# Head maxima subtracted on TensorE, small GpSimd work moved, FFN rounding on the way out of PSUM, and new order tables

## The chip, the core and the metric

The kernel runs on one core of one Trainium2 chip. The metric is device time in microseconds (us). A core has five instruction streams that run beside each other and meet only at semaphores: TensorE (PE, matmuls; its weight loads are listed apart as PEld), VectorE (DVE), ScalarE (ACT), GpSimd (POOL), and SyncE (SP), which here only issues DMAs.

## What is computed

The input is 16 batches of 128 tokens x 128 channels, with a context of the same shape. Four layers follow one another, each added to the running `x` behind a tanh gate. The first is an attention whose softmax runs over the 16 heads (`axis=1`), not over the keys, so every score has to be divided by a sum over heads. The second is a mixture of 8 experts of which each token uses two (the kernel computes all eight and weighs them). The third attends to the context with three kinds of products and joins four pieces through `W_l`. The fourth is an FFN whose activations are rounded to whole numbers up to 127 and whose weights are rounded to -1, 0, 1.

```python
# layer 1 (16 heads of 8 channels)
score = jnp.einsum('bhij,bhkj->bhik', k, q) / jnp.sqrt(jnp.asarray(dh, k.dtype))
attn = jax.nn.softmax(score, axis=1)
out = jnp.einsum('bhik,bhij->bhjk', attn, v)
...
# layer 3
x = jnp.concatenate([c, c2q_att, c * c2q_att, c * q2c_att], axis=-1)
z = x @ W_l.T + b_l
...
# layer 4
scale = 127.0 / jnp.clip(jnp.max(jnp.abs(x), axis=-1, keepdims=True), 1e-05)
xq = jnp.clip(jnp.round(x * scale), -128.0, 127.0) / scale
```

## The kernel before

The work is cut into 8 pairs of two batches (256 tokens). A pair goes through the four layers, whose tiles and steps begin with `a_` (and `head_`), `m_`, `f_` and `g_`. What each engine does, and in which order, is written out by hand: the table `WHEN` gives every step of every pair a number, `ONCE` the steps that run once, and `order(engine)` sorts an engine's steps by them. The engine walks that list from front to back; semaphores hold a step until its inputs are there. A step that waits therefore holds everything behind it on its engine. The numbers interleave the pairs: the attention of one pair stands among the experts of the pair before, the third layer of that one, and the FFN of the one before it.

Scores are made in four units to a pair, each 128 keys x 16 heads x 64 queries, and each fills both banks of the one PSUM tile `ps_sc`. For one unit: PE makes 16 small matmuls (L1234); DVE takes the maximum over heads (`head_max`, L1584) and subtracts it on the way to SBUF (`shifted`, L1590), which sets `s_shift` and so frees `ps_sc` for the next unit; ACT takes the exponential (`attn`, L1046); POOL adds up the heads as a tree of four steps (L939); DVE takes the reciprocal (L1606); POOL multiplies (L945); PE forms the weighted values (L1196). For units 1 and 3 of pair 0, DVE adds up the heads instead (L1598).

The rows of queries and keys that L1234 reads go through DRAM: SP stores three bf16 parts of each (L791) and then fetches them back as `k_rows` and `q_rows` (L799); the first unit of a pair waits for both.

The expert tiles are made by L1188 to L1190 (three fp32r products of 256 columns per tile), a GELU-like activation on ACT and DVE, and L1448. Every layer norm ends in `rstd()` on POOL: four instructions on 128x2 values (L843, L844, L846, L848). POOL also turns the two best experts into probabilities (`top_probs`, L885 to L894), and forms `y_res` = `y` + the bias of `W_l` (L912) which L1728 adds to the third layer. In the FFN, ACT adds a large constant `ROUND` that makes the float round (`g_r` L1143, `g_pr` L1165), a second pass takes it off and writes bf16 (`g_q` on DVE, L1750; `g_pq` on ACT, L1172), PE transposes these (L1373, L1399), and ACT copies them out of PSUM (`g_qt` L1152, `g_pt` L1181). The last pair has no work of a next pair beside it. Spare matmuls that feed nothing (L1205, L1213) stand at the start and at the end.

## Time and profile before

| | |
|---|---|
| Time, median of 3 runs | 398.3 us (397.81 to 398.43) |
| Span of the profiled execution | 397.3 us |
| Busy: PE / DVE / ACT / POOL | 324.9 / 313.1 / 256.4 / 299.1 us |
| Chain that ended last, share by engine | PE 37%, POOL 25%, DVE 13%, issue 10%, ACT 7%, DMA 4%, SP queue 3% |
| First transposes of the experts' input (L1243), pair 0 and pair 7 | 56.2 and 333.4 us |

The span runs from the first to the last instruction of one profiled execution. Busy times add up what an engine spent in instructions; those of PE overlap each other, because matmuls are pipelined. The chain is followed back from the last instruction, at each step to what released it. The last line gives the beat of the loop: seven periods lie between pair 0 and pair 7.

### The profile page before, as it was taken

To read this page: it belongs to the slowest core of one execution; us is meant where nothing else is said; L and a number is where in the kernel's file an instruction comes from. 1 tells how busy PE (TensorE), PEld (TensorE's weight loads), DVE (VectorE), ACT (ScalarE), POOL (GpSimd) and SP (SyncE) were. 2 spreads that over 40 slices of the span, in tenths; PEclk is the share of its full clock that TensorE was granted. 3 is DMA by queue.
4 is the path that set the end of the run, shared out by engine and by line. 5 is a ranking of instruction groups with operands and counts; after the bars stand their busy time and mean duration, and the time that the engine had idled before them with its cause. 6 is when DMAs were issued, how large, how long until landed. Compare 5 with 4: busy or idle time off the path is not lost.

```text
span 397.3 us, 10407 instructions
## 1 busy us (share of the span) xinstructions
PE 324.9 (82%) x3326; PEld 284.0 (71%) x3326; DVE 313.1 (79%) x913; ACT 256.4 (65%) x726; POOL 299.1 (75%) x459
## 2 busy tenths in 40 slices
PE   1365589898999789979998899879978997996875
PEld 1255469787898679867986698669957896994742
DVE  2679877598869997999799979995989678778434
ACT  4335254536846797779667885777658855875754
POOL 4378989799898989898999799988778873443010
PEclk9999767999999999999999999998999999999585
DMA  5967210300341114012401221204100000000000
GB/s 161 289 192 210 81 36 21 116 17 16 88 115 34 29 41 128 19 56 63 108 15 47 68 87 29 61 6 131 33 16 1 28 15 2 2 29 14 2 13 13
DMA packets 34454, 24.17 MB, mean 61 GB/s; under 512 B 3617, under 2 KB 32097, under 8 KB 34401
## 3 DMA queue, kind: packets, MB, share of 16 engines
q1 hardware_dynamic: 33680, 23.32, 19.7%
q8 instruction: 27, 0.44, 0.5%
q10 hardware_dynamic: 720, 0.20, 0.2%
q14 instruction: 27, 0.21, 0.2%
HBM read 16.16 MB, written 7.34 MB: 59 GB/s over the span
## 4 chain that ended last, share of the span: by engine, by line
PE 37%; POOL 25%; DVE 13%; issue 10%; ACT 7%; DMA 4%; SPq 3%; POOLq 0%; DVEq 0%; ACTq 0%
POOL tree L939 9%; PE ps_d L1448 8%; POOL attn L945 8%; PE ps_z L1188 4%; PE ps_a L1196 3%; PE ps_z L1189 3%; PE ps_z L1190 3%; POOL m_h L876 2%; DVE head_max L1584 2%; DMA wf_raw<-in_wd 2%; DVE m_u L1623 1%; DMA k_rows<-rows_dram 1%; DVE y L1655 1%; PE ps_sc L1234 1%; DVE shifted L1590 1%
## 5 line engine op out<-in xcount | busy, mean ns | idle before, releaser
L1188 PE MATMUL ps_z<-m_xhi,w_hi 128*128 128x256 f32 x240 | 76.9, 320 | 12.7 <-DVE m_h L1631 6.1
L945 POOL TENSOR_TENSOR attn<-attn,head_inv 128x1024 f32<-128x1024 f32 x32 | 75.8, 2371 | 0.2 <-DVE head_inv L1606 0.2
L1448 PE MATMUL ps_d<-wdn,m_h 128*128 128x128 f32 x512 | 71.4, 283 | 4.7 <-DVE m_h L1631 2.1
L1448 PEld LDWEIGHTS ps_d<-wdn,m_h 128*128 128x128 f32 x512 | 63.1, 194 | 8.5 <-issue 4.1
L1189 PE MATMUL ps_z<-m_xhi,w_lo 128*128 128x256 f32 x240 | 68.8, 287 | 0.0
L1190 PE MATMUL ps_z<-m_xlo,w_hi 128*128 128x256 f32 x240 | 68.6, 286 | 0.0
L1623 DVE SCALAR_TENSOR_TENSOR m_u<-m_tanh,ps_z 128x256 f32<-128x256 f32 x120 | 49.0, 411 | 17.6 <-ACT m_tanh L1033 16.7
L1033 ACT ACTIVATE m_tanh<-ps_z 128x256 f32<-128x256 f32 x120 | 45.9, 384 | 26.0 <-PE ps_z L1190 25.6
L1188 PEld LDWEIGHTS ps_z<-m_xhi,w_hi 128*128 128x128 f32 x240 | 46.7, 195 | 19.3 <-issue 6.1
L876 POOL TENSOR_TENSOR m_h<-m_u,m_z 128x256 f32<-128x256 f32 x56 | 41.1, 734 | 17.2 <-DVE m_u L1623 17.2
L939 POOL TENSOR_TENSOR tree<-tree 128x256 f32<-128x256 f32 (+2 forms) x90 | 46.4, 515 | 7.1
L1189 PEld LDWEIGHTS ps_z<-m_xhi,w_lo 128*128 128x128 f32 x240 | 46.9, 196 | 0.0
L1190 PEld LDWEIGHTS ps_z<-m_xlo,w_hi 128*128 128x128 f32 x240 | 46.7, 195 | 0.0
L939 POOL TENSOR_TENSOR tree<-attn 128x512 f32<-128x512 f32 x30 | 38.3, 1277 | 6.5 <-ACT attn L1046 6.3
L1584 DVE TENSOR_REDUCE head_max<-ps_sc 128x64 f32<-128x1024 f32 x32 | 38.9, 1215 | 4.5 <-PE ps_sc L1234 4.2
L1046 ACT ACTIVATE attn<-shifted 128x1024 f32<-128x1024 f32 x32 | 33.7, 1055 | 10.1 <-DVE shifted L1590 10.1
L1590 DVE TENSOR_TENSOR shifted<-ps_sc,head_max 128x1024 f32<-128x1024 f32 x32 | 38.8, 1213 | 0.3
L1655 DVE SCALAR_TENSOR_TENSOR y<-ps_d,weights,y 128x128 f32<-128x128 f32 x96 | 28.8, 342 | 4.5 <-PE ps_d L1448 3.1
L1631 DVE TENSOR_TENSOR m_h<-m_u,ps_z 128x256 f32<-128x256 f32 x67 | 27.6, 414 | 5.8 <-PE ps_d L1448 5.1
L1031 ACT ACTIVATE m_z<-ps_z 128x256 f32<-128x256 f32 x53 | 20.2, 381 | 14.6 <-PE ps_z L1190 13.8
L1196 PE MATMUL ps_a<-attn,v_diag 128*32 128x128 f32 x512 | 20.4, 290 | 3.7 <-POOL attn L945 3.3
L1234 PE MATMUL ps_sc<-q_rows,k_rows 48*128 48x64 bf16 x512 | 13.7, 196 | 7.7 <-DVE shifted L1590 5.6
(311 smaller groups left out, 852.0 us busy)
## 6 DMA issues: line engine op xcount, KB each, us to landing
rows_dram<-qk_parts SPq DMA_DIRECT2D x16, 192.0 KB, 2.2
k_rows<-rows_dram SPq DMA_DIRECT2D x16, 192.0 KB
q_rows<-rows_dram SPq DMA_DIRECT2D x16, 192.0 KB
w_raw<-in_w SPq DMA_DIRECT2D x2, 1024.0 KB, 7.9
rows_dram<-qk_parts SPq DMA_DIRECT2D x16, 128.0 KB, 2.0
x_in<-in_x SPq DMA_DIRECT2D x8, 128.0 KB, 2.4
ct_in<-in_ctx_t SPq DMA_DIRECT2D x8, 128.0 KB, 2.4
rows_dram<-qk_parts SPq DMA_DIRECT2D x16, 64.0 KB, 1.7
```

What stands on the lines that cost most here:

```text
L876: pool.tensor_tensor(m_h[:, k % 4], m_u[:, k % 4], m_z1[:, n % 3], ALU.mult).then_inc(s_mhp, 1)
L939: pool.tensor_tensor(dst, src[:, 0:n, :], src[:, n:2 * n, :], ALU.add).then_inc(s_tree, 1)
L945: pool.tensor_tensor(e, e, head_inv[:, u % 2].unsqueeze(1).to_broadcast([P, HEADS, HALF]), ALU.mult).then_inc(s_attn, 1)
L1033: act.activation(m_tanh[:, k % 2], tile_bank(p, k)[:, 0:TOK], ACT.Tanh, scale=0.5).then_inc(s_mt, 1)
L1046: act.activation(attn[:, b, :, k0:k0 + HALF], shifted[:, u % 2], ACT.Exp).then_inc(s_exp, 1)
L1188: pe.matmul(dst, hi_w, hi_x, start=start, stop=False)
L1189: pe.matmul(dst, lo_w, hi_x, start=False, stop=False)
L1190: return pe.matmul(dst, hi_w, lo_x, start=False, stop=True)
L1448: last = pe.matmul(ps_d[:, b * P:(b + 1) * P], m_h[:, m % 4, b * P:(b + 1) * P], wdn[:, m], start=(k == 0), stop=(k == TPE - 1))
L1584: dve.tensor_reduce(head_max[:, u % 2], sc.rearrange("p h k -> p k h"), AX.X, ALU.max).then_inc(s_hmax, 1)
L1590: dve.tensor_tensor(shifted[:, u % 2], sc, head_max[:, u % 2].unsqueeze(1).to_broadcast([P, HEADS, HALF]), ALU.subtract).then_inc(s_shift, 1)
L1623: dve.scalar_tensor_tensor(m_u[:, k % 4], m_tanh[:, k % 2], 1.0, z[:, 0:TOK], ALU.add, ALU.mult).then_inc(s_mu, 1)
```

## The change

The scores stay in PSUM. The unit's first matmul into each bank opens an accumulation that is left open; DVE takes the maximum with its sign turned (`head_nmax`), ACT rounds it to fp32r (`head_hi`), DVE takes the rest (`head_lo`), and PE adds both parts to every head by four matmuls of 512 columns against an identity (`pe.shift`). ACT then takes the exponential straight out of PSUM. `shifted` is gone, and the next unit's scores wait for the exponential (`s_exp`) instead of `s_shift`.

On POOL, `rstd()` keeps only the power; the addition of epsilon and the product go to DVE. `top_probs` goes to DVE, with a reciprocal in place of a power, and the expert weights are formed in two instructions instead of five. `y_res` is gone: PE adds the bias as one more bf16 product, whose DMA moves to `w_out`, and `y` gets a second buffer. In the FFN `g_q` and `g_pq` are gone: PE transposes `g_r` and `g_pr` in fp32, `ROUND` still in them, and the copy out of PSUM takes it off (`g_qt`, now on DVE; `g_pt` on ACT). All numbers of `WHEN` and `ONCE` are new; the table's first two lines stand for the rest.

```diff
 WHEN = {
-    "sp.load_a": (12, 1501, 2546, 3638, 7464, 12475, 17304, 20931),
+    "sp.load_a": (1, 705, 1778, 3447, 7009, 9104, 14876, 18102),
...
-                        wait(pe, s_shift, p.count(4, u))
+                        wait(pe, s_exp, p.count(4, u))
...
-                                                 start=True, stop=True, tile_position=(hq * HALF, 0))
+                                                 start=(hp == 0), stop=False, tile_position=(hq * HALF, 0),
+                                                 skip_group_check=True)
                         last.then_inc(s_score, 1)
+                    if p := due(now, "pe.shift", u):
+                        pe.wait_ge(s_nlo, p.count(4, u + 1))
+                        for hq in range(2):
+                            for part in (head_hi, head_lo):
+                                last = pe.matmul(ps_sc[:, hq], ident_r[:],
+                                                 part[:, u % 2].unsqueeze(1).to_broadcast([P, HEADS // 2, HALF]),
+                                                 start=False, stop=(part is head_lo), skip_group_check=True)
+                        last.then_inc(s_shift, 1)
...
-                        dve.tensor_reduce(head_max[:, u % 2], sc.rearrange("p h k -> p k h"), AX.X,
-                                          ALU.max).then_inc(s_hmax, 1)
-                    if p := due(now, "dve.head_shift", u):
...
+                        dve.tensor_reduce(head_nmax[:, u % 2], sc.rearrange("p h k -> p k h"), AX.X,
+                                          ALU.max, negate=True).then_inc(s_hmax, 1)
+                    if p := due(now, "dve.head_lo", u):
...
+                        dve.tensor_tensor(head_lo[:, u % 2], head_nmax[:, u % 2], head_hi[:, u % 2].bitcast(F32),
+                                          ALU.subtract).then_inc(s_nlo, 1)
...
+                    if p := due(now, "act.head_hi", u):
...
+                        act.activation(head_hi[:, u % 2], head_nmax[:, u % 2], ACT.Copy).then_inc(s_nhi, 1)
...
-                        act.activation(attn[:, b, :, k0:k0 + HALF], shifted[:, u % 2], ACT.Exp).then_inc(s_exp, 1)
+                        act.activation(attn[:, b, :, k0:k0 + HALF], ps_sc[:].rearrange("p a (h k) -> p (a h) k", k=HALF),
+                                       ACT.Exp).then_inc(s_exp, 1)
...
-                pool.tensor_tensor(rs[:, 0], mv[:, :, 1], eps_col[:], ALU.add).then_inc(s_rs, 1)
-                pool.tensor_tensor(rs[:, 1], mv[:, :, 0], minus_ones[:], ALU.mult).then_inc(s_rs, 1)
...
-                pool.tensor_tensor(rs[:, 3], rs[:, 2], rs[:, 1], ALU.mult).then_inc(s_rs, 1)
+                pool.tensor_tensor(rs[:, 0], rs[:, 2], minus_half[:], ALU.pow).then_inc(s_rs, 1)
...
+                dve.tensor_scalar(rs[:, 2], mv[:, :, 1], EPS, None, ALU.add).then_inc(s_rs, 1)
...
+                dve.scalar_tensor_tensor(rs[:, 1], mv[:, :, 0], -1.0, rs[:, 0], ALU.mult, ALU.mult).then_inc(s_rs, 1)
...
-                    pool.tensor_tensor(y_res[:], y[:], bl_all[:].unsqueeze(1).to_broadcast([P, 2, P]),
-                                       ALU.add).then_inc(s_fyb, 1)
...
+            def first_products(p, b):
+
+                s = slice(b * P, (b + 1) * P)
+                pe.matmul(late_bank(p, b)[:, s], ones_bf[:], bias_parts[:, 2], start=True, stop=False)
+                pe.matmul(late_bank(p, b)[:, s], f_ct[:, s], wl[:, 0], start=False, stop=False)
+                pe.matmul(late_bank(p, b)[:, s], f_c2q[:, s], wl[:, 1], start=False, stop=False)
...
-                            last = pe.transpose(batch_bank(p, b)[:, k * HALF:(k + 1) * HALF].bitcast(BF16),
-                                                g_pq[:, b, k * P:(k + 1) * P], ident_bf[:])
+                            last = pe.transpose(batch_bank(p, b)[:, k * P:(k + 1) * P],
+                                                g_pr[:, b, k * P:(k + 1) * P], ident[:])
...
-                        act.activation(g_pq[:, b], g_pr[:, b], ACT.Copy, bias=-ROUND).then_inc(s_gpq, 1)
...
-                        act.activation(g_pt[:, b], batch_bank(p, b)[:, 0:TOK].bitcast(BF16), ACT.Copy).then_inc(s_gpts, 1)
+                        act.activation(g_pt[:, b], batch_bank(p, b)[:], ACT.Copy, bias=-ROUND).then_inc(s_gpts, 1)
```

What the new numbers move is seen in the order of the instructions themselves. On SP, at the start of the program, before; `wf_raw` is the FFN's weights, `wcq`, `bsum` and `bl_all` small constants of the third layer, `rows_dram` the stores of the score rows:

```order
L770 DMA wf_raw<-in_wd 128x4x128
L763 DMA wcq<-in_w_cq 128x1
L763 DMA wcq<-in_w_q 128x1
L763 DMA wcq<-in_w_c 128x1
L765 DMA bsum<-in_b_cq 128x1
L765 DMA bsum<-in_b_q 128x1
L765 DMA bsum<-in_b_c 128x1
L766 DMA bl_all<-in_bl 128x128
L791 DMA rows_dram<-qk_parts 128x3x256
L791 DMA rows_dram<-qk_parts 128x2x256
L791 DMA rows_dram<-qk_parts 128x256
```

And the same place after:

```order
L788 DMA wf_raw<-in_wd 128x4x128
L822 DMA x_res<-in_x 128x2x128
L775 DMA gains<-in_g_xattn 128x2
L776 DMA gains<-in_g_ffn 128x2
L778 DMA bias_raw<-in_bv 96x128
L778 DMA bias_raw<-in_bo 96x128
L778 DMA bias_raw<-in_bl 96x128
L779 DMA wo_t<-in_wo 128x128
L797 DMA x_in<-in_x 128x2x128
L799 DMA ct_in<-in_ctx_t 128x2x128
L809 DMA rows_dram<-qk_parts 128x3x256 x2
```

The small constants went behind the stores; the output weights, and the inputs of pair 1, now stand ahead of them, and the stores of keys and queries follow one another.

On PE in pair 4, around the second unit of scores, before (`ps_z`, `ps_d`: expert tiles and their way down):

```order
L1196 MATMUL ps_a<-attn,v_diag 32x128 x8
L1448 MATMUL ps_d<-wdn,m_h 128x128 x4
L1234 MATMUL ps_sc<-q_rows,k_rows 128x64 x16
L1188 MATMUL ps_z<-m_xhi,w_hi 128x256
L1189 MATMUL ps_z<-m_xhi,w_lo 128x256
L1190 MATMUL ps_z<-m_xlo,w_hi 128x256
```

After, the four added matmuls of the first unit of pair 4, and what stands next to them (L1395 is the transposes of `g_pr`):

```order
L1395 MATMUL ps_g<-ident,g_pr 128x128 x4
L1444 MATMUL ps_d<-wdn,m_h 128x128 x4
L1235 MATMUL ps_sc<-head_hi,ident_r 128x512
L1235 MATMUL ps_sc<-head_lo,ident_r 128x512
L1235 MATMUL ps_sc<-head_hi,ident_r 128x512
L1235 MATMUL ps_sc<-head_lo,ident_r 128x512
L1172 MATMUL ps_z<-m_xhi,w_hi 128x256
L1173 MATMUL ps_z<-m_xhi,w_lo 128x256
L1174 MATMUL ps_z<-m_xlo,w_hi 128x256
```

In this unit, 25 rows of other work stand on PE between the scores and the four added matmuls, and 16 rows between these and the scores of the second unit, where before 18 rows stood between the two units' scores. On ACT, at the end of the program, before:

```order
L1165 ACTIVATE g_pr<-g_p,round_col,g_ps 128x512
L1167 ACTIVATE g_ps<-g_pmc,cg 128x1
L1172 ACTIVATE g_pq<-g_pr 128x512
L1165 ACTIVATE g_pr<-g_p,round_col,g_ps 128x512
L1167 ACTIVATE g_ps<-g_pmc,cg 128x1
L1172 ACTIVATE g_pq<-g_pr 128x512
L1181 ACTIVATE g_pt<-ps_g 128x512
L1181 ACTIVATE g_pt<-ps_d 128x512
```

And after:

```order
L1154 ACTIVATE g_pr<-g_p,round_col,g_ps 128x512
L1156 ACTIVATE g_ps<-g_pmc,cg 128x1
L1154 ACTIVATE g_pr<-g_p,round_col,g_ps 128x512
L1156 ACTIVATE g_ps<-g_pmc,cg 128x1
L1165 ACTIVATE g_pt<-ps_g 128x512
L1165 ACTIVATE g_pt<-ps_d 128x512
```

Two of the eight instructions are gone; the rest keep their order.

## Rows read from the trace of the kernel before

**Rows 1.** Stretches: start to end, length, busy us of PE, PEld, DVE, ACT, POOL, clock.
```profile
175.00:215.00 40.00, 35.85 (x389) 31.67 (x388) 35.50 (x110) 30.51 (x89) 36.81 (x58) 1.00 0.21 59
...
340.00:397.00 57.00, 44.92 (x305) 35.39 (x304) 33.67 (x118) 37.02 (x111) 14.53 (x31) 0.82 0.04 13
```

**Rows 2.** Waits of POOL from 135 to 255 us: total, times, longest.
```profile
POOL m_h L876 <- DVE m_u L1623: 3.2, 3, 1.4
...
POOL attn L945 <- DVE head_inv L1606: 0.2, 1, 0.2
```

**Rows 3.** Chain that ended last, 140 to 165 us: start, us, what.
```profile
149.05 2.01 DMA rows_dram<-qk_parts
...
153.26 5.63 DMA k_rows<-rows_dram
...
158.93 0.41 PE ps_sc L1234 x16
...
159.67 0.95 PE ps_d L1448 x8
160.62 0.12 PE ps_z L1188
...
162.38 0.57 PE ps_a L1196 x16
```

**Rows 4.** Timeline of SP, start of the program: start, us, line, tiles.
```profile
9.60 0.44 SPq L770 DMA_DIRECT2D wf_raw<-in_wd  x1
...
19.98 1.52 SPq L799 DMA_DIRECT2D k_rows<-rows_dram  x2
```

**Rows 5.** DMA issues of the first 30 us: KB each, us to landing.
```profile
wf_raw<-in_wd SPq DMA_DIRECT2D x1, 256.0 KB, 6.6
```

**Rows 6.** Timeline of DVE, the score units of pair 0.
```profile
28.15 1.23 DVE L1584 TENSOR_REDUCE head_max<-ps_sc 128x64 f32<-128x1024 f32 x1 [0.52 <-PE ps_sc L1234]
...
39.53 1.22 DVE L1584 TENSOR_REDUCE head_max<-ps_sc 128x64 f32<-128x1024 f32 x1
```

**Rows 7.** Waits of PE from 20 to 57 us.
```profile
PE ps_sc L1234 <- DVE shifted L1590: 5.6, 4, 1.7
```

**Rows 8.** Groups by line and shape, 135 to 255 us, three pairs: total, mean ns.
```profile
L1584 DVE TENSOR_REDUCE head_max<-ps_sc 128x64 f32<-128x1024 f32 x12 | 14.6, 1219 | 1.0 <-PE ps_sc L1234 0.8
L1590 DVE TENSOR_TENSOR shifted<-ps_sc,head_max 128x1024 f32<-128x1024 f32 x12 | 14.6, 1213 | 0.0
...
L1046 ACT ACTIVATE attn<-shifted 128x1024 f32<-128x1024 f32 x12 | 12.6, 1053 | 0.0
...
L912 POOL TENSOR_TENSOR y_res<-y,bl_all 128x256 f32<-128x256 f32 x3 | 2.2, 731 | 0.0
...
L846 POOL TENSOR_TENSOR g_rs<-g_rs,minus_half 128x2 f32<-128x2 f32 x3 | 2.1, 702 | 0.0
```

**Rows 9.** Timeline of PE alone, 379 to 382 us: 512-column matmuls.
```profile
381.22 0.38 PE L1205 MATMUL ps_f<-wf_q,ident_bf 128*128 128x512 bf16 x1
381.43 0.38 PE L1205 MATMUL ps_z<-wf_q,ident_bf 128*128 128x512 bf16 x1
```

**Rows 10.** Timeline of all engines, 379 to 385 us.
```profile
380.55 0.20 POOL L843 TENSOR_TENSOR g_rs<-g_mv,eps_col 128x2 f32<-128x2 f32 x1 [4.07 <-DVE g_mv L1493]
...
381.63 0.20 POOL L848 TENSOR_TENSOR g_rs<-g_rs 128x2 f32<-128x2 f32 x1
...
383.28 0.17 DVE L1739 TENSOR_SCALAR g_amc<-g_amax 128x2 f32<-128x2 f32 x1
...
384.41 0.54 DVE L1750 TENSOR_SCALAR g_q<-g_r 128x128 bf16<-128x128 f32 x2 [0.63 <-ACT g_r L1143]
384.59 0.28 ACT L1147 ACTIVATE g_sc<-g_amc,cg 128x2 f32<-128x2 f32 x1
```

**Rows 11.** Timeline of all engines, 387 us to the end.
```profile
392.29 0.61 ACT L1172 ACTIVATE g_pq<-g_pr 128x512 bf16<-128x512 f32 x1
...
392.95 0.61 PE L1399 MATMUL ps_d<-ident_bf,g_pq 128*128 128x128 bf16 x4 [0.41 <-ACT g_pq L1172]
```

More of the change, by code:

```diff
@@ L372 @@
+    "dve.top_probs": (
[3 rows of a table added]
+    ),
+    "dve.top_eq": (5568, 8861, 12616, 16374, 20213, 24255, 27628, 31034),
+    "dve.g_qt": (11383, 14725, 18977, 22777, 26686, 30156, 33027, 35064),
+    "act.head_hi": (
[4 rows of a table added]
+    ),
+    "dve.head_lo": (
[4 rows of a table added]
+    ),
+    "pe.shift": (
[4 rows of a table added]
     ),
@@ L602, in build @@
         f_w4 = sb("f_w4", [P, 2, P])
-        y_res = sb("y_res", [P, 2, P])
         x3s = sb("x3", [P, 2, 2, P])
@@ L1147, in _ @@
                     act.activation(g_sc[:, :, 1], g_amc[:], ACT.Identity, scale=cg[:, 0:1]).then_inc(s_gsz, 1)
-                if p := due(now, "act.g_qt"):
-                    wait(act, s_gu, p.before().count(4, 4))
-                    for g in groups(p):
-                        act.wait_ge(s_gqt, p.count(1, 1) + g[0])
-                        act.activation(g_qt[:, cols(g)], batch_bank(p, g[0])[:, g[0] * HALF:(g[-1] + 1) * HALF].bitcast(BF16),
-                                       ACT.Copy).then_inc(s_gqs, 1)
                 for u in range(4):
```

512 lines of the change are left out of this document (256 added, 256 removed), and 279 rows, old and new, of the table WHEN.

## The prediction

> **What bounds the kernel now.** I read the 40-us stretches first, then the waits of the fullest engine, then the chain that ended last, then the start and the end of the program line by line.
>
> In the steady part POOL is the full engine: 36.81 us busy of 40 [rows 1]. From 135 to 255 us, three pairs, its waits are five rows with 6.2 us in all, the first and last of them in [rows 2]: 2.1 us per pair. The beat is (333.4 - 56.2) / 7 = 39.6 us by the two starts of L1243 in the table of times. So the full engine's beat is its own work with the small gaps between its instructions, 37.5 us, and 2.1 us of waits that nothing fills.
>
> PE looks as full (35.85 us), but its busy times overlap. The chain shows what an instruction really takes of PE: 0.12 us for a 256-column product, 0.95 us for the eight passes of L1448, 0.57 us for 16 weighted values, 0.41 us for a unit's scores [rows 3]. A pair has 96, 8, 4 and 4 of these: 11.5 + 7.6 + 2.3 + 1.6 = 23.0 us. Some 90 further instructions (projections, third layer, FFN, transposes) at 0.1 to 0.12 us make it about 33 us, an estimate from those rows. PE has some 6.5 us per pair to spare.
>
> The Trainium skill says that matmul busy time is a bad measure of how near PE is to its limit, because matmuls are pipelined (Trainium Kernel Development and Optimization, Performance Expectations). The trace agrees: 0.12 us in the chain. By busy times the change would give PE 42 us per pair and the kernel would be some 17 us slower; I don't count so.
>
> Score rows are a second path. Where a pair's rows are late, the chain runs through a store of 2.01 us, SP's issues, and a fetch whose last part takes 5.63 us [rows 3].
>
> **The start.** The last large load is issued at 9.60, and it lands 6.6 us later, at 16.2 [rows 4, 5]. The first fetch is issued at 19.98 and the first maximum starts at 28.15 [rows 4, 6]. The change puts the row stores ahead of seven small loads and lets the query stores follow the key stores, but puts about 0.32 MB more of other loads ahead of them. No earlier than the big loads allow: 16.2 + 2.0 (store) + 8.2 (fetch to maximum, 28.15 - 19.98) = 26.4 with nothing added, and 1 to 1.5 us more if the added loads are queued ahead. So the gain lies between 0 and 2; I take -1.5.
>
> Then the units of pair 0 follow each other on one tile of PSUM. Before, a unit held `ps_sc` for scores, maximum and subtraction. The four maxima run from 28.15 to 39.53, 3.8 us apart [rows 6], and PE waited 5.6 us for `shifted` there [rows 7]. After, a unit holds `ps_sc` until the exponential ends: scores 0.41, maximum 1.22, `head_hi` about 0.28 and `head_lo` about 0.20 (a small ACT operation takes 0.28, a small DVE one 0.17 [rows 10]), four matmuls at 0.22 each, exponential 1.05, and six hand-overs of some 0.08: 4.5 us [rows 3, 8, 9]. Three intervals: +2.2. Some of it is hidden, as POOL was also a bound of these units. Start in all: **+0.7**, between -2 and +2.5.
>
> **POOL in the loop.** Each of four `rstd` loses three instructions of 0.195 us (0.20 in [rows 10]): 2.3 us. `top_probs` loses four such and a power of 0.70 [rows 8]: 1.5 us. `y_res` loses 0.73 [rows 8]. With the gaps between them, 5 us per pair. POOL falls to about 32.5 of 39.6 and is no longer the full engine. That is no gain of 5 us, because PE becomes the next.
>
> **PE in the loop.** Sixteen added matmuls of 512 columns. The trace has no fp32r ones of that size; nearest are bf16 ones of 512, which follow each other 0.21 us apart (381.22 to 381.43 [rows 9]), and fp32r ones of 256 at 0.12 [rows 3], twice which is 0.24. I take 0.22: 3.5 us, between 3.4 and 3.8, plus some 0.1 per unit for changing the kind of matmul. Ten transposes go from bf16 to fp32: 0.04 to 0.08 more each, 0.6 us. The bias adds 0.15. In all +4.5: about 37.5 us per pair, just what POOL's own work was.
>
> **DVE and ACT.** DVE loses four `shifted` of 1.213 us [rows 8], `g_q` and three weight instructions; it gains four `head_lo`, eight norm operations, `g_qt` and five small ones, most near the 0.17 of [rows 10]: about -2.5 us net, an estimate, on an engine with 35.5 busy [rows 1]. ACT loses `g_qt` and two `g_pq` and gains four `head_hi`: -0.5. The exponential from PSUM I hold at 1.05; a tenth more or less would not count. Neither engine bounds the loop, but both now stand inside each unit's chain: `head_hi` and `head_lo` wait their turn behind expert work.
>
> The loop's sum: PE as the full engine with 37.5, and the waits that the full engine had, 2.1, would be 39.6, no change. But DVE and POOL, the engines that PE mostly waits for, become emptier, which should take some tenths off the waits. I take 39.3, -0.3 per pair, **-2.1** over seven periods. The bounds are waits of 0.5 us (38.0) and of 2.8 us (40.3).
>
> **The end.** From 340 us to the end no engine is full, and PE's clock is granted at 0.82 on average [rows 1]; the chain is serial. Between `g_r` and the transposes, `g_q` (384.41, two parts in 0.54 [rows 10]) goes: -0.3. The last `g_pq` (392.29, 0.61) goes, and the transposes behind it get longer: in bf16 four take 0.61 there [rows 11], in fp32 perhaps 0.9: -0.3 to -0.6 net. `rstd` at 380.55 took until 381.83 on POOL alone [rows 10]; DVE, POOL, DVE with two hand-overs is 0.17 + 0.70 + 0.2 + 0.15: -0.05. ACT no longer has the `g_pq` of pair 6 between steps of the third layer of pair 7: about -0.5. `y_res` was hidden there. These are -1.2 to -1.5; the spare matmuls are set anew, and each us of PE's chain there that is granted the full clock in place of half of it gives 0.5 back, so I take **-2.0**, between -3.5 and 0.
>
> **Sum.** +0.7 - 2.1 - 2.0 = -3.4 on a span of 397.3: 393.9. The median of the runs is 1.0 us above that span (398.3), so 394.9.
>
> **Rivals.**
> - *Much faster: PE's waits fill up.* POOL came to 36.81 busy of 40 in one stretch [rows 1], so an order can fill an engine almost wholly. With PE's waits at 0.6 us the beat is 38.1: 7 x -1.5 = -10.5. With -2 at the end and 0 at the start: 384.8 + 1.0 = 386. For it: three engines lose work. Against: PE's inputs come from all the others, and the fetch of rows takes 7 us or more whoever is full.
> - *Slower: the units of scores hold PE up.* In place of one wait (`shifted`), a unit now crosses PE, DVE, ACT, DVE, PE, ACT, and PE stands in order at the four matmuls and again at the next unit's scores. If each unit costs PE 0.2 us more that nothing fills, the waits are 2.9 and the beat is 40.4: 7 x 0.8 = +5.6. With +0.7 and -2.0: 401.6 + 1.0 = 402.6. It decides from 2.1 us of unfilled waits per pair on. For it: the 5.6 us that PE already waited for `ps_sc` [rows 7]. Against: in the loop, 25 rows of other work stand between scores and the added matmuls in the unit that I read, about 4 us, more than maximum, `head_hi` and `head_lo` need.
> - The Trainium skill asks that independent groups of matmuls rotate through different banks of PSUM, so that one is emptied while the next is made (Perfetto Trace Analysis, Matmuls). The change holds the one tile longer. By that rule alone this rival wins; the 5.6 us of [rows 7] agree with it for the start, where PE has nothing else to do, and no row shows it for the loop.
> - *No change:* the loop at 39.6 and the end's gain eaten by the start: 397.3 + 0.7 - 1.5 = 396.5 and up, 397.5 to 399.
>
> **How the numbers follow.** The forecast (390 to 397.5) gets 0.41, much faster (below 390) 0.20, no change 0.12, slower 0.27. A measurement of this kernel tells about 0.2%, 0.8 us, from no change: below 397.5 is faster (0.61), above 399.1 slower (0.27). For 8 in 10 the range goes from 384, a little beyond the fast rival, to 404, a little beyond the slow one.
>
> **What would show it.** The starts of the experts' first transposes in pairs 0 and 7: the beat should be 38.8 to 39.6. POOL near 32 us busy per 40, with waits several times those of before. PE's added matmuls 0.21 to 0.24 us apart in the chain; if they are 0.4 apart, PE has 3 us more per pair and the slow rival wins. The first maximum at 26 to 27 us, units of pair 0 about 4.5 us apart. PE's waits in the loop: for `head_lo` or for the exponential, more than 0.5 us per pair together would speak for the slow rival; near nothing, with the beat at 38, for the fast one. From the last x of the third layer to the end some 0.8 us less. I am wrong if PE's real work is not near 37.5, or if the first rows come more than 2 us earlier or later than I have it.

## The result, and the profile after

The changed kernel takes 432.2 us against 398.1 us for the kernel before on the same chip: a ratio of 1.085, 95% interval 1.080 to 1.091. Times in this document are medians of the runs within 1.5% of a kernel's fastest; with all runs, one of 1106 us among them, the changed kernel's median is 433.4, the figure from which the expectations below start (as they do from 436.8 for e4). The prediction was 394.9, so even its sign was wrong. Only one of its three terms, the end, came out.

The first transposes of the experts' input (now also L1243) cut the profiled execution, with a span of 428.6 us, into the prediction's three parts. Those of pair 0 start at 69.8 us and those of pair 7 at 366.6. Start: 69.8 - 56.2 = +13.5 (forecast +0.7). Loop: a beat of (366.6 - 69.8) / 7 = 42.4 in place of 39.6, +19.7 (forecast -2.1). End: 62.0 in place of 63.9, -1.9 (forecast -2.0). Together +31.3, the difference of the two spans. (PE's timeline after, at the two places:)

```profile
69.76 0.44 PE L1243 MATMUL ps_d<-ident,m_xn 128*128 128x128 f32 x2 [1.89 <-ACT m_xn L985]
...
366.61 0.44 PE L1243 MATMUL ps_d<-ident,m_xn 128*128 128x128 f32 x2
```

Here are the stretches of the changed kernel (columns: stretch and its length, then busy time and instructions of PE, PE's weight loads, DVE, ACT, POOL, then the granted clock, DMA share, GB/s):

```profile
20.00:30.00 10.00, 5.97 (x52) 5.49 (x53) 5.09 (x16) 3.61 (x7) 5.47 (x4) 0.50 0.50 139
30.00:55.00 25.00, 17.80 (x189) 14.03 (x186) 16.14 (x26) 8.75 (x18) 14.43 (x13) 0.70 0.20 56
...
175.00:215.00 40.00, 33.94 (x332) 29.93 (x331) 37.40 (x100) 24.60 (x71) 27.47 (x32) 0.96 0.20 60
```

and the kernel before in the first two of these stretches:

```profile
20.00:30.00 10.00, 6.32 (x69) 5.48 (x69) 7.19 (x13) 3.77 (x10) 7.42 (x8) 1.00 0.63 188
30.00:55.00 25.00, 15.56 (x278) 13.14 (x278) 21.45 (x33) 9.74 (x18) 21.93 (x29) 0.86 0.40 121
```

In the steady part POOL fell from 36.81 [rows 1] to 27.47 us of 40, as forecast. But PE, which should have taken its place, is at 33.94, and DVE, which should have become 2.5 us lighter, rose to 37.40 and is now the fullest. An engine that is given less work and is longer busy is where one should look. The groups of DVE between 60 and 340 us show it (total us, then mean ns of one):

```profile
L1499 DVE SCALAR_TENSOR_TENSOR m_rs<-m_mv,m_rs 128x2 f32<-128x2 f32 x7 | 11.9, 1695 | 0.4 <-POOL m_rs L860 0.3
L1610 DVE TENSOR_TENSOR head_lo<-head_nmax,head_hi 128x64 fp32r<-128x64 f32 x26 | 9.8, 377 | 0.4 <-ACT head_hi L1034 0.3
...
L1499 DVE SCALAR_TENSOR_TENSOR f_rs<-f_mv,f_rs 128x2 f32<-128x2 f32 x6 | 5.5, 918 | 0.1
...
L1494 DVE TENSOR_SCALAR a_rs<-a_mv 128x2 f32<-128x2 f32 x5 | 3.9, 785 | 0.1
L1494 DVE TENSOR_SCALAR g_rs<-g_mv 128x2 f32<-128x2 f32 x5 | 3.5, 704 | 0.1
...
L1494 DVE TENSOR_SCALAR m_rs<-m_mv 128x2 f32<-128x2 f32 x7 | 1.2, 165 | 0.2
```

Two numbers per partition, and a mean of 1.7 us. An addition on as many numbers of the same tile (the last row) takes 0.165. A mean hides how it comes about, so here is one of them with its neighbours (timeline of DVE, POOL and ACT, around the middle norm of pair 0; start, us, and in brackets the idle time before it and who ended it):

```profile
65.74 0.70 POOL L860 TENSOR_TENSOR m_rs<-m_rs,minus_half 128x2 f32<-128x2 f32 x1 [0.43 <-DVE m_rs L1494]
...
66.41 2.37 POOL L935 TENSOR_TENSOR attn<-attn,head_inv 128x1024 f32<-128x1024 f32 x1
...
66.47 2.32 DVE L1499 SCALAR_TENSOR_TENSOR m_rs<-m_mv,m_rs 128x2 f32<-128x2 f32 x1 [0.27 <-POOL m_rs L860]
...
68.83 0.88 ACT L985 ACTIVATE m_xn<-x,m_rs 128x128 f32<-128x128 f32 x2 [1.37 <-DVE m_rs L1499]
```

DVE's little product begins 0.06 us after POOL's large multiplication and ends 0.01 us after it, at 68.79 against 68.78. Its shortest run takes 0.15. ACT stands 1.37 us for it, and by about so much the experts' input is late. The place makes it likely: the product waits for POOL's power, and POOL's next instruction begins just when the power ends. The lengths over the whole execution (min/median/max ns):

```profile
L1499 DVE SCALAR_TENSOR_TENSOR m_rs<-m_mv,m_rs x8: 151/2067/2319, 66.5 to 364.0; 128x2 f32<-128x2 f32 x8
...
L1610 DVE TENSOR_TENSOR head_lo<-head_nmax,head_hi x32: 155/224/1290, 30.1 to 341.3; 128x64 fp32r<-128x64 f32 x32
...
L1605 DVE TENSOR_REDUCE head_nmax<-ps_sc x32: 1159/1215/1225, 28.6 to 339.0; 128x64 f32<-128x1024 f32 x32
...
L1688 DVE RECIPROCAL tinv<-tsum x8: 150/162/166, 82.6 to 374.4; 128x2 f32<-128x2 f32 x8
...
L1769 DVE TENSOR_REDUCE g_amax<-g_h x8: 385/408/421, 142.6 to 415.1; 128x2 f32<-128x256 f32 x8
```

What reads PSUM (L1605) never stretches. What reads one SBUF tile as a reduction or reciprocal (L1769, L1688) does not either. What reads two SBUF tiles does, and so do some steps that join one tile with a constant or a column (L1494, up to 2.03 us). I call the excess over the shortest of the same form, where it is above 0.3 us, DVE's **standing**. Added up over the execution it is 43.4 us after and 2.1 us before; 9.1 us of it are in DVE's 37.40 of the stretch above. It comes from 45 instructions, and each of them overlaps an instruction of POOL and ends 0.01 to 0.15 us after it.

The Trainium skill has this as a rule: DVE and GpSimd share a pair of SBUF ports, a DVE instruction with two SBUF inputs contends for it with a GpSimd instruction that reads SBUF, one in a two-port mode with any, and whichever is issued second blocks until the first is done (SBUF — State Buffer, Who interferes with whom). The trace agrees: 45 of 45 end with POOL's instruction. The rule spoke against this change, and the prediction did not weigh it.

The other side of it is POOL, which now waits for DVE (POOL's waits, 60 to 340 us: total, times, longest; [rows 2] has those of before):

```profile
POOL m_h L888 <- DVE m_u L1642: 21.4, 17, 2.3
POOL f_rs L860 <- DVE f_rs L1494: 10.7, 6, 3.0
POOL tree L929 <- ACT attn L1040: 10.2, 8, 4.1
POOL m_rs L860 <- DVE m_rs L1494: 6.1, 5, 2.2
```

So three theories stood after the result. *Standing*: DVE blocked by POOL's instructions. *Late in the order*: a norm that was four POOL instructions in a row now goes DVE, POOL, DVE, and the engine that walks a fixed list stands for whoever is late. *Units*: the rival on record, the one PSUM tile held until the exponential. A fourth, smaller one was the clock: 0.50 and 0.70 between 20 and 55 us, where the kernel before had 1.00 and 0.86. A granted clock of 0.50 is the lower of the two levels (1.2 of 2.4 GHz) for the whole stretch; just before, up to 20.21 us, PE had stood 6.5 us for `ct_lo` (4.2 us in the kernel before).

### The profile page after: what moved, and what is told of

Same layout as the page of the kernel before. It is cut to its first block and busy times, and to the rows that moved or that the text cites. A ratio compares the mean times of both kernels' runs of the same rounds, so it can differ in the third digit from the quotient of the medians.

```text
span 428.6 us, 10656 instructions
## 1 busy us (share of the span) xinstructions
PE 362.1 (84%) x3470; PEld 316.1 (74%) x3470; DVE 333.1 (78%) x992; ACT 253.2 (59%) x733; POOL 267.3 (62%) x313
## 5 line engine op out<-in xcount | busy, mean ns | idle before, releaser
L1172 PE MATMUL ps_z<-m_xhi,w_hi 128*128 128x256 f32 x240 | 75.4, 314 | 3.3 <-DVE m_xlo L1629 1.5
L888 POOL TENSOR_TENSOR m_h<-m_u,m_z 128x256 f32<-128x256 f32 x56 | 40.8, 733 | 37.9 <-DVE m_u L1642 35.8
L1642 DVE SCALAR_TENSOR_TENSOR m_u<-m_tanh,ps_z 128x256 f32<-128x256 f32 x120 | 48.8, 413 | 19.1 <-ACT m_tanh L1023 18.6
L1605 DVE TENSOR_REDUCE head_nmax<-ps_sc 128x64 f32<-128x1024 f32 x32 | 38.8, 1213 | 13.3 <-PE ps_sc L1225 13.3
L1040 ACT ACTIVATE attn<-ps_sc 128x1024 f32<-128x1024 f32 x32 | 32.8, 1025 | 22.3 <-PE ps_sc L1235 22.2
L1235 PE MATMUL ps_sc<-head_hi,ident_r 128*128 128x512 f32 x64 | 30.5, 477 | 4.9 <-DVE head_lo L1610 4.5
L1235 PE MATMUL ps_sc<-head_lo,ident_r 128*128 128x512 f32 x64 | 27.7, 434 | 0.0
```

The source lines that it names most:

```text
L888: pool.tensor_tensor(m_h[:, k % 4], m_u[:, k % 4], m_z1[:, n % 3], ALU.mult).then_inc(s_mhp, 1)
L1040: act.activation(attn[:, b, :, k0:k0 + HALF], ps_sc[:].rearrange("p a (h k) -> p (a h) k", k=HALF), ACT.Exp).then_inc(s_exp, 1)
L1172: pe.matmul(dst, hi_w, hi_x, start=start, stop=False)
L1235: last = pe.matmul(ps_sc[:, hq], ident_r[:], part[:, u % 2].unsqueeze(1).to_broadcast([P, HEADS // 2, HALF]), start=False, stop=(part is h ...
L1605: dve.tensor_reduce(head_nmax[:, u % 2], sc.rearrange("p h k -> p k h"), AX.X, ALU.max, negate=True).then_inc(s_hmax, 1)
L1642: dve.scalar_tensor_tensor(m_u[:, k % 4], m_tanh[:, k % 2], 1.0, z[:, 0:TOK], ALU.add, ALU.mult).then_inc(s_mu, 1)
```

## The experiments

"Start" is the first L1243 (or the line that answers to it), "beat" the mean distance of the next seven. Start, beat and standing are read from the traced run, which took 439.2 us in e4, 418.5 in e13 and 405.2 in e14, more than the times in their rows. The kernel before gave 398.1 to 399.3 beside these runs.

| run | kernel | us | ratio to before, 95% | start, beat | standing |
|---|---|---|---|---|---|
| before | | 398.1 | | 56.2, 39.6 | 2.1 |
| after | | 432.2 | 1.080 to 1.091 | 69.8, 42.4 | 43.4 |
| e1 | after, small norm steps on ACT and POOL | 423.7 | 1.061 to 1.072 | 68.4, 41.0 | 20.8 |
| e2 | after, only `head_hi` subtracted | 426.7 | 1.067 to 1.075 | 66.1, 42.5 | 37.5 |
| e3 | after, more spare matmuls at the start | 431.1 | 1.076 to 1.090 | 66.5, 42.9 | 42.3 |
| e5 | e1 + e2 + e3 | 408.8 | 1.022 to 1.029 | 62.7, 40.1 | 16.9 |
| e10 | e5 without the added matmuls | 406.8 | 1.015 to 1.025 | 61.9, 39.7 | 15.1 |
| e12 | e5, top-two back on POOL | 419.0 | 1.045 to 1.053 | 62.8, 41.4 | 15.0 |
| e15 | after, POOL's multiplication in four | 413.6 | 1.032 to 1.039 | 67.3, 40.7 | 25.6 |
| e18 | e15 + e2 + e3 | 407.1 | 1.014 to 1.024 | 63.3, 40.3 | 23.1 |
| e19 | e5, POOL's multiplication in four | 413.2 | 1.026 to 1.039 | 63.4, 40.8 | 13.3 |
| e4 | before, small norm steps on DVE | 432.8 | 1.080 to 1.093 | 61.2, 44.9 | 28.0 |
| e11 | before, small norm steps on ACT | 414.2 | 1.031 to 1.042 | 56.9, 41.8 | 3.4 |
| e13 | e11, bias on PE | 411.8 | 1.027 to 1.043 | 58.5, 41.9 | 3.3 |
| e14 | e11, ACT's steps earlier in its order | 401.2 | 1.003 to 1.009 | 55.6, 40.4 | 2.3 |
| e16 | before, top-two on DVE | 410.2 | 1.017 to 1.032 | 56.0, 41.2 | 8.1 |
| e17 | before, POOL's multiplication in four | 410.7 | 1.019 to 1.033 | 57.7, 41.4 | 6.7 |
| e6 | before, FFN part alone | 402.5 | 1.007 to 1.013 | 56.4, 40.0 | 1.9 |
| e7 | before, score part alone, two parts | 450.4 | 1.126 to 1.135 | 73.1, 44.2 | 14.5 |
| e8 | the same, one part | 423.1 | 1.055 to 1.068 | 65.9, 41.9 | 5.3 |

### Standing: the norms' place

Two runs move the small steps of the norm. In the changed kernel they go off DVE (e1: epsilon and negated mean to ACT, the product to POOL); in the kernel before they go onto DVE as in the changed kernel, with nothing else changed (e4).

```diff
 # e1, against after (ACT; POOL then multiplies rs[:, 0] by rs[:, 3])
-dve.tensor_scalar(rs[:, 2], mv[:, :, 1], EPS, None, ALU.add)
-dve.scalar_tensor_tensor(rs[:, 1], mv[:, :, 0], -1.0, rs[:, 0], ALU.mult, ALU.mult)
+act.activation(rs[:, 2], mv[:, :, 1], ACT.Copy, bias=EPS)
+act.activation(rs[:, 3], mv[:, :, 0], ACT.Copy, scale=-1.0)
```

> The changed kernel, but the small steps of the layer norms no longer on DVE: epsilon and the negated mean go to ACT (at DVE's old place in the order), the power and the last product stay on POOL. Theory 1 (standing DVE): DVE operations that read and write SBUF alone stand until the POOL instruction under way ends, 43.4 us in all in the changed kernel, 26 us of it in the norms; these 26 go, and with them some 1 to 1.5 us per pair and 1.5 us at the start: 418 to 424 us instead of 433.4. Theory 2 (units): the loop is longer because each unit of scores crosses PE, DVE, ACT, DVE, PE, ACT on one PSUM tile; then nothing changes here: 430 to 435.

> The kernel before, with only the split of the norms added: epsilon and the last product on DVE, POOL keeps the power. Theory 1 (standing DVE): DVE gets some 20 us of standing in POOL's shadow, which eats what POOL gains: 400 to 408 us against 398. Rival (POOL bounds the loop and DVE pays only the 0.17 us of each operation): POOL loses 2.3 us per pair, 386 to 394 us.

e1 gave 423.7, 8.5 us less, and half of the standing. e4 gave 432.8, beyond both expectations: this one edit makes the kernel before as slow as the whole change does. Its counterpart e11, the same steps on ACT, gave 414.2 with 3.4 us of standing.

```diff
 # e11, against before
-pool.tensor_tensor(rs[:, 0], mv[:, :, 1], eps_col[:], ALU.add)
-pool.tensor_tensor(rs[:, 1], mv[:, :, 0], minus_ones[:], ALU.mult)
+act.activation(rs[:, 0], mv[:, :, 1], ACT.Copy, bias=EPS)
+act.activation(rs[:, 1], mv[:, :, 0], ACT.Copy, scale=-1.0)
```

> The kernel before, with only this: epsilon and the negated mean of the norms go from POOL to ACT, power and last product stay on POOL. The counterpart of the split that put them on DVE (436.8 us): the same two hand-overs of POOL's first steps, but to an engine that doesn't stand in POOL's shadow. Theory 1 (standing DVE): no loss, and POOL, which bounds the loop, gets 1.6 us per pair shorter: 388 to 396 us. Rival (the hand-over between engines that work in order is what costs): 405 to 430.

DVE's groups in e4, 60 to 340 us, look like those of the changed kernel:

```profile
L1507 DVE SCALAR_TENSOR_TENSOR m_rs<-m_mv,m_rs 128x2 f32<-128x2 f32 x7 | 11.7, 1674 | 0.8 <-POOL m_rs L852 0.7
...
L1507 DVE SCALAR_TENSOR_TENSOR g_rs<-g_mv,g_rs 128x2 f32<-128x2 f32 x5 | 7.6, 1510 | 0.6 <-POOL g_rs L852 0.6
```

The difference of 18.6 us between e4 and e11 goes with the standing (28.0 against 3.4). But e11 is itself 15 us slower than before, with POOL relieved of two instructions per norm and nearly no standing. That is the second cause.

### Standing: the length of POOL's instruction

If DVE stands exactly for the POOL instruction under way, shorter instructions on POOL must shorten it, though POOL has no less to do. e15 cuts the 2.37-us multiplication into four; e17 makes the same cut in the kernel before and so says what the cut costs.

```diff
-pool.tensor_tensor(e, e, head_inv[:, u % 2].unsqueeze(1).to_broadcast([P, HEADS, HALF]), ALU.mult)
+for k in range(4):
+    h = slice(k * HEADS // 4, (k + 1) * HEADS // 4)
+    nx = pool.tensor_tensor(e[:, h], e[:, h], head_inv[:, u % 2].unsqueeze(1)
+                            .to_broadcast([P, HEADS // 4, HALF]), ALU.mult)
```

> The changed kernel with POOL's multiplication of attn by the reciprocal sum (128x1024, 2.37 us, the longest instruction of POOL) cut into four of 128x256 (0.73 us is what POOL's other 128x256 instructions take, so the four take about 2.9). Theory A (a small DVE instruction stands until the POOL instruction under way has ended): no DVE instruction that coincided with attn stands over 0.8 us any more; the longest of m_rs falls from 2.32 to about 1.3 (the 128x512 tree add is left), and the sum of DVE's standing from 43.4 to 22 to 30 us. The time: -5 to -8 us by that, +2 to +8 for the longer POOL work, so 425 to 436 us. Rival B (DVE stands until POOL has a pause, or for any other reason than the one instruction): the sum stays above 38 us, and the time rises by POOL's longer work alone, 434 to 441 us.

> The kernel before with the same cut of POOL's multiplication into four of 128x256: what the cut costs by itself. DVE stands 2.1 us in all in the kernel before, so there is nothing to gain. POOL is given 0.5 us more a unit, 2 us a pair: 402 to 412 us if POOL's time shows in full or in part (eight pairs); 398 to 399 us if the pieces run into one another and the cut is free.

Timeline of POOL and DVE in e15, a middle norm that meets the multiplication, and the lengths of that instruction:

```profile
268.25 2.80 POOL L937 TENSOR_TENSOR attn<-attn,head_inv 128x256 f32<-128x256 f32 x4
...
268.32 0.68 DVE L1502 SCALAR_TENSOR_TENSOR m_rs<-m_mv,m_rs 128x2 f32<-128x2 f32 x1
```
```profile
L1502 DVE SCALAR_TENSOR_TENSOR m_rs<-m_mv,m_rs x8: 150/544/685, 65.4 to 349.2; 128x2 f32<-128x2 f32 x8
```

POOL works on for 2.80 us, DVE is released after the first quarter. The median fell from 2.07 to 0.54 us and the longest from 2.32 to 0.69; the standing came to 25.6, inside what was expected of standing and far below the rival's 38. The time fell by 18.6 us, to 413.6, more than I had expected. In the kernel before the same cut costs 11.7 us; POOL, the full engine there, gets 0.43 us more per unit (2.80 in place of 2.37). So the changed kernel gained though it was given more work: the clearest evidence for the mechanism.

### Late in the order

e11 had almost no standing and yet was 15 us slower. POOL's waits in e11 (60 to 340 us):

```profile
POOL m_rs L847 <- ACT m_rs L962: 8.0, 6, 3.5
...
POOL g_rs L847 <- ACT g_rs L962: 7.9, 5, 2.4
POOL a_rs L847 <- ACT a_rs L962: 5.8, 3, 3.6
...
POOL f_rs L847 <- ACT f_rs L962: 2.0, 2, 1.1
```

POOL, the full engine, stands 23.7 us for 0.2-us steps that are queued behind other work of ACT. e14 moves these steps forward in ACT's list, right behind DVE's statistics; not one instruction differs (one of the four lines is shown).

```diff
-"act.m_eps": (5247, 8737, 12685, 16864, 20950, 25150, 29310, 33192),
+"act.m_eps": (5170, 8639, 12643, 16760, 20740, 25015, 29256, 33150),
```

> The kernel before with epsilon and negated mean of the four norms on ACT, as in the run with 414.2 us, but the two small instructions stand in ACT's order right behind DVE's statistics (0.4 to 5 us earlier for most, up to 17 us for the attention's norm), so that ACT, not POOL, waits for what is late. In the run with 414.2 us POOL stood 23.7 us in 60:340 us for these two (m_rs 8.0, g_rs 7.9, a_rs 5.8, f_rs 2.0). Theory A (it is the place in a fixed order that costs): POOL stands under 8 us for them and the time comes to 402 to 408 us. Theory B (the hand-over costs wherever it stands, because now ACT stands for DVE and passes its lateness on): POOL's wait falls too, but ACT's for the statistics comes to over 8 us, and the time stays at 411 to 418 us.

The same waits in e14:

```profile
POOL m_rs L847 <- ACT m_rs L962: 7.8, 5, 3.0
...
POOL g_rs L847 <- ACT g_rs L962: 2.2, 3, 1.7
```

401.2 us, 13.0 less, by order alone; POOL's waits for these steps fell to about 10, not to the 8 I had asked for. So most of the cost lay not in the hand-over but in its place in the order. Yet nothing was won over before (+0.6%) by taking eight small instructions a pair off the full engine.

The bias on PE was put on top of e11 (e13), and the top-two probabilities were moved both ways: onto DVE in the kernel before (e16) and back onto POOL in e5 (e12).

```diff
 # e13, against e11 (y_res is gone)
-pool.tensor_tensor(y_res[:], y[:], bl_all[:].unsqueeze(1).to_broadcast([P, 2, P]), ALU.add)
+the three bf16 parts of bl * tanh are one more product in first_products(), as in after
 # e16, against before; e12 is the reverse, against e5
-pool.tensor_tensor(tsum[:], texp[:], ones[:, 0:2].unsqueeze(2), ALU.add)      # and four more
+dve.tensor_scalar(tsum[:], texp[:], 1.0, None, ALU.add)                       # and reciprocal, two products
```

> The kernel before with the norms' first steps on ACT and, of the change, the bias of the third layer on PE (no y_res on POOL, two buffers of y). Theory (POOL bounds the loop): another 0.7 us per pair off POOL, 1 to 4 us less than with the norms alone, so 386 to 394. Rival (PE and DVE are the next bound at once): equal to the run with the norms alone within 1 us.

> The kernel before with only the probabilities of the two chosen experts moved from POOL (five small instructions, 1.5 us a pair) to DVE, written as in the changed kernel; the last part of the change that has not been run alone. Theory A (small work on DVE costs more than it saves on POOL, by standing and by being late): DVE stands 4 to 10 us in all, the time is 400 to 406 us. Rival B (here the move pays, as the sum before the run had it: POOL was the fullest engine): 393 to 397.5 us.

> The kernel with norms off DVE, one part and more spare matmuls (408.8 us), with the top-two probabilities back on POOL and the expert weights in five instructions on DVE as before. Theory 1: of the 16.9 us that DVE still stands there, some 9 go; 402 to 406 us. Rival (POOL's 1.5 us per pair and its waits weigh as much): 408 to 412.

The bias is worth nothing that can be seen (411.8 against 414.2, with runs of e13 from 411.0 to 416.9). The top-two steps lose either way: +11 us onto DVE in before's order, +10 us back onto POOL in the changed order. In e12 only 1.9 of the 9 us of standing that were expected to go went, and DVE waits 7.1 us for `tprob` from POOL: both of its expectations failed. In e16 the standing is 8.1 us as expected, but the time is above both of my expectations: POOL's waits for `m_u` rose from 10.0 to 17.8 us and for the exponential from 4.1 to 11.0. An order made for one placement pays for another one.

### Units, rounding and clock

e2 leaves `head_lo` out of the changed kernel; e7 and e8 put the new score units into the kernel before, whose tables were stretched by 12 us where a unit needs it; e10 takes e5 and leaves the subtraction of the maximum out. e6 is the FFN part alone, and e3 adds 69 groups of spare matmuls in the first 60 us.

```diff
 # e2, against after; e8 against e7 likewise (e10: no pe.shift at all)
-for part in (head_hi, head_lo):
-    last = pe.matmul(ps_sc[:, hq], ident_r[:], part[:, u % 2]..., start=False, stop=(part is head_lo))
+last = pe.matmul(ps_sc[:, hq], ident_r[:], head_hi[:, u % 2]..., start=False, stop=True)
 # e6, against before (and g_pq likewise)
-last = pe.transpose(batch_bank(p, b)[:, b * HALF:(b + 1) * HALF].bitcast(BF16), g_q[:, b], ident_bf[:])
+last = pe.transpose(batch_bank(p, b)[:, b * P:(b + 1) * P], g_r[:, b], ident[:])
```

> The changed kernel with the fp32r part head_hi alone subtracted: no head_lo, two added matmuls per unit in place of four. The softmax over heads doesn't depend on what is subtracted as long as it is the same for all heads. Theory 1 (standing DVE): head_lo's standing (4.4 us) and its own 7 us go from DVE, 426 to 430 us. Theory 2 (units): each unit gets about 0.9 us shorter (two matmuls 0.45, head_lo 0.22, a hand-over), 3.6 us per pair where units follow each other: 408 to 418 us.

> The kernel before, with only the score part: scores kept open in PSUM, head_hi on ACT, head_lo on DVE, four added matmuls per unit, exponential from PSUM; the numbers of the order tables are stretched by 12 us in all so that the new steps fit between the old ones. Theory 2 (units hold PE up): 405 to 415 us. Rival (DVE loses 3.7 us per pair, the longer unit is hidden): 392 to 398. Standing of head_lo alone (theory 1) would add 4 to 8 us of DVE in either case.

> As the run before it, but with one part (head_hi) subtracted by two matmuls per unit: no head_lo on DVE. Theory 2: 5 to 8 us less than with two parts, so 398 to 408. Rival (the unit is hidden): within 2 us of the two-part kernel.

> The kernel before, with only the FFN part: g_r and g_pr transposed in fp32 and rounded while leaving PSUM, g_qt on DVE, no g_q, no g_pq. Theory: ACT and DVE lose work that is hidden in the loop, and the serial end loses some 0.7 to 1.5 us: 396 to 398 us. Rival: the fp32 transposes and g_qt at the place of ACT's copy in DVE's order cost the loop more than that: 399 to 403.

> The changed kernel with 69 more spare groups of matmuls on PE in the first 60 us, where PE waits (24 before pair 1's first projection, 10 before the first scores, 14 before pair 1's scores, the others between the units). Theory 3 (clock): the start, 13.5 us longer than before, is partly due to the granted clock of 0.50 at 20 to 30 us and 0.70 at 30 to 55 us; with it at 0.9 or more the four matmuls of a unit take 0.9 instead of 1.7 us: 3 to 5 us less, 428 to 430. Theories 1 and 2: no change, 432 to 435.

e7 and e8 are the worst and the third worst of the kernels made from before (450.4 and 423.1): put in alone, the longer unit costs far more than the rival on record had it. PE's waits in e7 name it, and so does the time of `head_lo` in the middle of the unit (14.6 us for 26, in place of 26 times 0.16):

```profile
PE ps_sc L1264 <- DVE head_lo L1618: 12.4, 17, 1.7
PE ps_sc L1254 <- ACT attn L1065: 5.6, 8, 1.1
```
```profile
L1618 DVE TENSOR_TENSOR head_lo<-head_nmax,head_hi 128x64 fp32r<-128x64 f32 x26 | 14.6, 561 | 12.5 <-ACT head_hi L1059 12.5
```

Without `head_lo` (e8) the standing falls from 14.5 to 5.3 us and the time by 27 us, where 5 to 8 were expected. The stretched order is a crude one, so 52 us is no price of the units as such. In the new order one part less is worth 5.5 us (e2): 426.7, within the 426 to 430 of the standing theory and far from the 408 to 418 of the units. The FFN part alone is worth +1.0% (e6): two passes fewer, and no gain in an order that had hidden them.

e3 brought the clock to 0.66, 0.93 and 0.96 in the stretches 20:30, 30:55 and 55:95, from 0.50, 0.70 and 0.81. The start came 3.3 us earlier, but the beat rose from 42.4 to 42.9 us, and the time fell by 1.1 us, less than the spread of the runs: in the total the clock is a small part at most.

### Do they add up?

> The changed kernel with the three earlier edits together: small norm steps off DVE, one part (head_hi) subtracted, more spare matmuls at the start. If the three causes are apart, the gains add: 433.4 - 9.7 - 6.7 - 2.3 = 414.7 us. If they hide each other's cost (an engine that stops standing meets another wait), 417 to 421. If standing DVE operations and long units together held the beat, it falls below 40 us per pair and the time to 405 or less.

> The kernel with norms off DVE, one part and more spare matmuls (408.8 us), now without the added matmuls: head_hi is still made, but not subtracted; the exponential is of the bare scores. Work left out: the subtraction. Theory 2 (each unit's way over the engines and PE's added work hold the loop): PE loses 1.9 us per pair and the unit one hand-over and 0.5 us: 393 to 400 us. Rival (what is left of the loss lies in the new order and in other DVE steps): 404 to 408.

> The changed kernel with three of the edits at once: POOL's multiplication cut into four, only head_hi subtracted (the lower part is left out, so the exponentials are off by the rounding of the maximum), and the spare matmuls of the start. The norms' small steps stay on DVE, where the change put them. By the single runs: 433.4 - 19.9 - 6.7 - 2.3 = 404.5 us. Theory A (three separate causes, each worth what it was alone): 402 to 408 us, with 18 to 24 us of DVE's standing left. Rival B (they are one cause seen three times: the standing comes out of the units): the gains overlap, 409 to 414 us.

> The same as the run beside it, with the norms' epsilon and negated mean on ACT and their product on POOL as well: the run with 408.8 us, with POOL's multiplication cut into four. Before it DVE stood 16.9 us there. Theory A (what is left of the standing is worth 0.5 us or more of time per us, and POOL, no longer full, hides the cut's 2 us a pair): DVE stands 8 to 11 us and the time is 403 to 408 us. Rival B (with the norms away POOL is near its bound and the cut costs what it cost in the kernel before, about 10 us): 410 to 418 us. If this is faster than the run beside it, the norms' place still matters with short POOL instructions.

By the times of the table the single gains are 8.5 (e1), 5.5 (e2), 1.1 (e3) and 18.6 us (e15). e18, with the cut, one part and the spare matmuls, gave 407.1, where these add up to 407.0: the three add. e5, with the norms' move in place of the cut, gave 408.8, where the sum gives 417.1: there the edits help each other. In e10, once the norms are away, the added matmuls themselves are worth 2 us, hardly more than the spread; that is the rival's range. e19 against e5: with the norms off DVE, the cut gains nothing (413.2 against 408.8, intervals that overlap), although the standing fell from 16.9 to 13.3. Neither theory in its expectation was right about the sizes, but the sign is rival B's. With short POOL instructions the norms are better off on DVE (407.1 in e18 against 413.2 in e19), with long ones off it (423.7 in e1 against 432.2 after).

What stays: e18 is 10.0 us longer in its span than before, 7.1 of it at the start, 4.8 in the loop and -1.9 at the end, and 23 us of standing are left in it. No run puts the new order beside the old work, or the old order beside all of the new, so what the order costs by itself is open. No kernel here is faster than the one before.

## Why the prediction was wrong

**DVE and ACT, the step that failed.** "It gains four `head_lo`, eight norm operations ... most near the 0.17 of [rows 10]". The price was read at the end of the program, where POOL has little to do. In the loop the middle norm's product takes 1.70 us in the mean, and 43.4 us of standing came in all. The prediction asked of each small step how long it takes and not beside what it runs. Over the seven periods DVE's busy time rose from 33.6 to 36.6 us per pair; without the standing (0.3 and 5.6 us) it fell from 33.4 to 31.0. So the "-2.5 us net" was right about the work, and the blocking, put at nothing without a reason, was more than twice as large. e4 and e15 show the step's weight: 432.8 by the norms alone, -18.6 us by shorter POOL instructions.

**POOL in the loop.** That POOL would fall to 32.5 was right in direction (27.5 of 40, at a longer beat; over the seven periods 31.3 us per pair in place of 34.7). "No longer the full engine" was right, too, and led astray: DVE became the full one, and e11 shows that a relieved POOL can give a longer beat. "Waits several times those of before" was named as a sign of success, and they came (POOL 21.4 for `m_u`, where it was 10.0, and 10.7 for `f_rs`); they were a part of the cost. The line "DVE, POOL, DVE with two hand-overs ... -0.05" held at the end of the program (1.14 us in place of 1.28) and not in the loop.

**PE in the loop.** The added matmuls are 0.23 us apart at a granted clock of 1.00 (186.8 to 188.0 us; forecast 0.22) and 0.43 at 0.50 (36.8 to 38.9 us, in the start; timelines of PE, first in the loop, then in pair 0):

```profile
187.17 0.39 PE L1235 MATMUL ps_sc<-head_lo,ident_r 128*128 128x512 f32 x1
187.40 0.40 PE L1235 MATMUL ps_sc<-head_hi,ident_r 128*128 128x512 f32 x1
```
```profile
37.47 0.63 PE L1235 MATMUL ps_sc<-head_lo,ident_r 128*128 128x512 f32 x1
37.90 0.63 PE L1235 MATMUL ps_sc<-head_hi,ident_r 128*128 128x512 f32 x1
```

The price was right, and PE being the next bound was wrong: even by busy times, which overlap, it is at 33.9 of 40. The first of the four is followed after 0.31 us (186.86 to 187.17), near the 0.1 per unit put down for changing the kind of matmul. Four fp32 transposes at the end took 0.66 us where four in bf16 took 0.61, not the 0.9 that was guessed.

**The start.** Forecast +0.7, measured +13.5. This is the second step that failed. The first fetch was issued 0.6 us earlier than before (19.43), yet the first maximum did not come 1.5 us earlier but 0.4 later (28.57), and the units of pair 0 are 6.2 us apart, not 4.5 (timelines of DVE and of POOL; [rows 6] are those of before):

```profile
28.57 1.23 DVE L1605 TENSOR_REDUCE head_nmax<-ps_sc 128x64 f32<-128x1024 f32 x1 [2.81 <-PE ps_sc L1225]
...
40.71 1.23 DVE L1605 TENSOR_REDUCE head_nmax<-ps_sc 128x64 f32<-128x1024 f32 x1 [1.72 <-PE ps_sc L1225]
41.85 1.52 DVE L1499 SCALAR_TENSOR_TENSOR a_rs<-a_mv,a_rs 128x2 f32<-128x2 f32 x1
43.30 0.21 DVE L1610 TENSOR_TENSOR head_lo<-head_nmax,head_hi 128x64 fp32r<-128x64 f32 x1
...
47.21 1.23 DVE L1605 TENSOR_REDUCE head_nmax<-ps_sc 128x64 f32<-128x1024 f32 x1 [0.46 <-PE ps_sc L1225]
```
```profile
41.02 2.34 POOL L935 TENSOR_TENSOR attn<-attn,head_inv 128x1024 f32<-128x1024 f32 x1
```

The working added up the unit at full clock with every engine free. Between 40.71 and 43.30 stands what it left out: `head_hi` is ready at 42.23, but DVE is in a norm's product that began at 41.85 and ends at 43.37 with POOL's multiplication (43.36). Added to this are the matmuls at 0.43.

The working also had no term for pair 1. The fetch of its rows is issued at 47.27 in place of 38.54: six small loads of constants now stand ahead of it on SP, and then SP stands 2.9 us for the scores of pair 0's fourth unit, because the program lets the tiles of rows be written again only then. Pair 1's first scores wait for that fetch and start at 54.63 in place of 46.73. The fetch after, what SP waited for between 30 and 52 us, the scores, and last the fetch before:

```profile
47.27 1.65 SPq L817 DMA_DIRECT2D q_rows<-rows_dram  x2
```
```profile
SPq L487 <- PE ps_sc L1225: 2.9, 1, 2.9
```
```profile
54.63 0.61 PE L1225 MATMUL ps_sc<-q_rows,k_rows 48*128 48x64 bf16 x16 [3.22 <-DMA k_rows<-rows_dram]
```
```profile
38.54 1.42 SPq L799 DMA_DIRECT2D k_rows<-rows_dram  x2
```

From there to the experts' input it is 15.1 us in place of 9.5, about 1.4 of it by the standing at 66.47 shown above. e2 and e3 each took over 3 us off the start. In e5, with both and e1, the fetch is issued at 42.39 and the start comes at 62.7, still 6.5 us late; no run takes that rest apart.

**The loop.** Forecast -0.3 per pair, measured +2.8. The 2.1 us of unfilled waits that the full engine had were carried over; they were a property of that order and that placement.

**The end.** Forecast -2.0, measured -1.9, of which 1.2 lie behind the last `x` of the third layer (17.9 us before, 16.8 after; 0.8 was the mark). The rest was put down to a missing `g_pq` of pair 6 and to spare matmuls, which no run tests, so the close hit is in part luck. And e6 shows that its parts don't carry over: in before's order the FFN part alone gained nothing.

**The rivals.** "Units of scores hold PE up" had the sign, at 402.6. By its own test it stays undecided: from 60 to 340 us PE waits 2.6 us for `head_lo` and 0.7 for the exponential, 0.5 per pair, just the mark. It is a part of the loss (e2, 5.5 us, and pair 0 in the start) and in the loop not the main one. No rival in the prediction had DVE blocked by POOL. The range, 384 to 404, rested on waits of PE between 0.5 and 2.8 us per pair, and so could not hold it either.

## What to carry to other kernels

Before moving small SBUF work from GpSimd to VectorE, look at what GpSimd runs at that moment: price the step at the length of the GpSimd instruction beside it, above all where the step waits for GpSimd and so tends to meet its next instruction (6 of 8 middle norms here). Shorten those instructions, or give the step to ScalarE; here either helped, and both together were slower than the first alone (e19 against e18). And where engines walk fixed lists, a step that crosses to another engine costs what is queued ahead of it there: read the new waits of the engine that used to do it all, and move the step in the list before judging the move.
